# Scores and weighted sums of a cross attention in plain float32 on tiles of TensorE, in place of products of high and low parts

## The reference, cut to what matters

```
q = query @ Wq.T + bq;  k = ctx @ Wk.T + bk;  v = ctx @ Wv.T + bv      # 16 heads of 32
scores = einsum('bhqd,bhkd->bhqk', q, k) / sqrt(32)
s = where(scores >= 0, scores + 1, 1 / (1 - scores))                   # "stablemax"
attn = s / sum(s, axis=-1)
context = einsum('bhqk,bhkd->bhqd', attn, v)
out = context @ Wo.T + bo
```

## Time and profile before

| | |
|---|---|
| median of 3 runs | 1409.66 us (1409.51 to 1411.08) |
| the profiled execution's own time | 1411.17 us |
| its span, first to last instruction | 1409.4 us |
| PE busy | 1381.0 us, 98% |
| DVE busy | 902.0 us, 64% |
| ACT busy | 810.5 us, 58% |
| POOL busy | 417.1 us, 30% |
| mean granted TensorE clock | 0.993 |

### The profile page before, as it was taken

The page is one execution under the profiler, slowest core; times in us unless marked ns, Lnnn a source line. Parts: engine busy times, 40 slices in busy tenths (PEclk is TensorE's granted clock), DMA queues, the critical chain, the costliest instruction groups (busy, mean ns, idle before and its releaser), DMA issues.

```text
span 1409.4 us, 23502 instructions
## 1 busy us (share of the span) xinstructions
PE 1381.0 (98%) x9278; PEld 1243.1 (88%) x9278; DVE 902.0 (64%) x1491; ACT 810.5 (58%) x1453; POOL 417.1 (30%) x214
## 2 busy tenths in 40 slices
PE   8999999999999999999999999989999999999998
PEld 6999999989889989789998988879898999989997
DVE  5556766756766766766675676575676644645565
ACT  4666667657556755756765756564654435545443
POOL 2344444353344444434435333420003101001000
PEclk9999999999999999999999999999999999999999
DMA  6120111111121111011101111085454669999991
GB/s 221 63 71 27 35 34 31 31 65 46 31 72 31 31 64 60 16 61 42 31 31 64 46 31 65 31 330 184 152 189 149 212 216 348 339 366 338 352 392 51
DMA packets 34855, 174.41 MB, mean 124 GB/s; under 512 B 6155, under 2 KB 8363, under 8 KB 18485
## 3 DMA queue, kind: packets, MB, share of 16 engines
q1 hardware_dynamic: 32996, 168.10, 33.2%
q0 software_dynamic: 1744, 4.76, 1.1%
HBM read 166.78 MB, written 6.06 MB: 123 GB/s over the span
## 4 chain that ended last, share of the span: by engine, by line
PE 88%; DVE 6%; ACT 4%; issue 1%; DMA 1%; PEldq 0%; SPq 0%; DVEq 0%; PEld 0%; ACTq 0%
PE bank L700 18%; PE bank L688 17%; PE bank L1017 10%; PE bank L720 10%; PE bank L1034 8%; PE bank L874 6%; PE po L733 6%; PE po L891 6%; DVE tt L1297 1%; PE bank L791 1%; PE bank L755 1%; PE bank L836 1%; DVE sa L1305 1%; ACT tt L1178 1%; DVE sa L1310 1%
## 5 line engine op out<-in xcount | busy, mean ns | idle before, releaser
L554 POOL TENSOR_TENSOR xn<-xn,tt 128x1024 f32<-128x1024 f32 x96 | 237.5, 2474 | 461.1 <-DVE sa L1310 461.1
L1405 DVE TENSOR_TENSOR wsl<-ring,wsh 128x2048 fp32r<-128x2048 f32 x72 | 165.0, 2291 | 112.6 <-ACT wsh L1118 112.5
L1278 DVE SCALAR_TENSOR_TENSOR kl<-bank,bkt,kh 128x256 fp32r<-128x256 f32 (+1 forms) x190 | 93.6, 493 | 200.9 <-ACT kh L1069 200.7
L688 PE MATMUL bank<-cxh,wkh 128*128 128x256 f32 (+1 forms) x752 | 215.5, 287 | 3.2 <-DVE va L1285 3.2
L688 PE MATMUL bank<-cxl,wkh 128*128 128x256 f32 (+1 forms) x752 | 215.6, 287 | 0.0
L688 PE MATMUL bank<-cxh,wkl 128*128 128x256 f32 (+1 forms) x752 | 215.4, 286 | 0.0
L1173 ACT ACTIVATE tt<-bank 128x512 f32<-128x512 f32 (+1 forms) x208 | 124.3, 599 | 84.5 <-PE bank L720 78.7
L700 PE MATMUL bank<-wvh,cxh 128*128 128x512 f32 (+1 forms) x416 | 165.1, 397 | 1.3 <-DVE kl L1278 1.3
L1118 ACT CAST wsh<-ring 128x2048 fp32r<-128x2048 f32 x72 | 137.4, 1908 | 46.6 <-PE po L891 23.1
L700 PE MATMUL bank<-wvl,cxh 128*128 128x512 f32 (+1 forms) x416 | 163.7, 394 | 0.0
L700 PE MATMUL bank<-wvh,cxl 128*128 128x512 f32 (+1 forms) x416 | 163.3, 392 | 0.0
(11 more groups left out here) (252 smaller groups left out, 2938.7 us busy)
## 6 DMA issues: line engine op xcount, KB each, us to landing
ring<-in_w SPq DMA_DIRECT2D x112, 1024.0 KB, 6.8
ctxt<-in_ctx SPq DMA_DIRECT2D x40, 512.0 KB, 3.5
ctxt<-in_ctx SPq DMA_DIRECT2D x8, 642.0 KB, 4.0
wqt<-in_wo SPq DMA_DIRECT2D x4, 1024.0 KB, 5.7
wqt<-in_aq SPq DMA_DIRECT2D x4, 1024.0 KB, 6.5
wqt<-in_ap_ SPq DMA_DIRECT2D x4, 1024.0 KB, 6.5
yrows<-K SPq DMA_DIRECT2D x1, 2048.0 KB, 8.7
tt<-in_wk SPq DMA_DIRECT2D x2, 512.0 KB, 5.4
```

Source lines behind the costliest of these rows:

```text
L554: e.tensor_tensor(dacc[0:kn, y, :], dacc[0:kn, y, :], tt[0:kn, w, :], ALU.add).then_inc(s["da_pool"], 1)
L688: m = e.matmul(dst[:, 0:n], (wkh, wkl)[a][:, c, g * P:(g + 1) * P], (cxh, cxl)[b][:, u, c, 0:n], start=(c == 0 and x_ == 0), stop=(c == 3 ...
L1405: e.tensor_tensor(wsl[m % 3][:], ring[slot(unit_split(m))][:], wsh[m % 3][:].bitcast(F32), ALU.subtract).then_inc(s["wl_dve"], 1)
```

## The change

- Keys, values and queries are kept as plain float32 (`kk`, `va`, `qb`); their high and low parts and the instructions of ACT and DVE that made them go. DVE reads key and value banks in one instruction each (`keys`, `values`), ACT writes the queries.
- Scores: two products for each group, of 64 rows each (two heads, 128 columns), the one on rows 0 to 63 into bank `scb[n % 2][0]`, the other on rows 64 to 127 into `scb[n % 2][1]`. There are two pairs of score banks; a chunk waits for the reading of the chunk two before.
- Weighted sums: for each group four products of 32 weight columns (one head) with 64 columns, each into its own 32 rows of one bank, `pob[b % 2]`. They read `tt` itself, so `sa` and its splitting go. `batch_low` and `batch_out` go; `normalised` reads the bank.
- `tt` has three buffers. POOL's sum waits for `f_dve`.
- Order on PE: scores, `attended` (both batches in one slot), `shared_up`, weighted sums, denominators, all key groups, values. The last two chunks' values come one slot later than before. The 18 and 36 products on ones go.
- The first three expert loads are issued in slot 92 in place of behind the loop, the first two splits in slots 100 and 103. Buffers are laid out anew for this.

```diff
@@ scores (pe)
-                for hb in range(2):
-                    if n:
-                        e.wait_ge(s["f_dve"], 2 * (n - 1) + hb + 1)
...
-                    for g in (2 * hb, 2 * hb + 1):
-                        dst = scb[hb][0:kn, 256 * (g % 2):256 * (g % 2) + 256]
-                        for x_, (a, c) in enumerate(three):
-                            m = e.matmul(dst, (kh, kl)[a][:, u, g, k * P:k * P + kn], (qbh, qbl)[c][:, b % 2, g, :],
-                                         start=(x_ == 0), stop=(x_ == 2))
-                    m.then_inc(s["s_pe"], 1)
+                if n >= 2:
+                    e.wait_ge(s["f_dve"], 2 * (n - 2) + 2)
...
+                for g in range(4):
+                    if k == 0:
+                        e.wait_ge(s["proj_read"], use["k", i, g] + 1)
+                    for j in range(2):
+                        r = slice(64 * j, 64 * j + 64)
+                        m = e.matmul(scb[n % 2][j][0:kn, P * g:P * g + P], kk[r, u, g, k * P:k * P + kn],
+                                     qb[r, b % 2, g, :], start=True, stop=True)
+                        if g == 3:
+                            m.then_inc(s["s_pe"], 1)
@@ weighted (pe)
-                if head and b:
-                    e.wait_ge(s["out_dve"], 8 * b)
-                for hb in range(2):
-                    e.wait_ge(s["sl_dve"], 2 * n + hb + 1)
-                    for p_ in (2 * hb, 2 * hb + 1, 2 * hb + 4, 2 * hb + 5):
-                        m = e.matmul(po[:, 256 * p_:256 * p_ + 256], va[0:kn, n % VR, P * p_:P * p_ + P],
-                                     sa[0:kn, w, 256 * p_:256 * p_ + 256], start=(head and p_ % 2 == 0),
-                                     stop=(tail and p_ % 2 == 1), skip_group_check=True)
+                e.wait_ge(s["f_dve"], 2 * n + 2)
+                if head and b >= 2:
+                    e.wait_ge(s["cr_dve"], normalised_by(b - 2))
+                for g in range(4):
+                    for h in range(4):
+                        m = e.matmul(pob[b % 2][32 * h:32 * h + 32, 64 * g:64 * g + 64],
+                                     va[0:kn, n % VR, P * g + 32 * h:P * g + 32 * h + 32],
+                                     weights_of(tt[0:kn, n % TR, :], g, h), start=(head and g == 0),
+                                     stop=(tail and g == 3), skip_group_check=True)
@@ order of a slot (pe)
+                if tile(n, 9) is not None:
+                    for b in range(2):
+                        attended(tile(n, 9), b)
+                if NCH <= n < NCH + 2 * NSH:
+                    shared_up(n - NCH)
+                if 1 <= n < NCH + 1:
+                    weighted(n - 1)
+                for b in finished(n)[0]:
                     denominators(b)
-                if n == NCH:
-                    warm(36, pj[use["v", NCH - 1] % 2])
-                if 1 <= n < NCH + 1 and (n - 1) % PER:
-                    weighted(n - 1)
-                for i, g in late:
+                for i, g in early + late:
                     keys(i, g)
@@ act: before the three operations on tt
-                    if n >= 2:
-                        e.wait_ge(s["da_pool"], n - 1)
+                    if n >= TR:
+                        e.wait_ge(s["da_pool"], n - TR + 1)
+                        e.wait_ge(s["p_pe"], n - TR + 1)
@@ vector
+            def keys(i, g):
...
+                e.tensor_scalar(kk[:, u, g, 0:n], key_bank(i, g)[:, 0:n], bkt[:, g:g + 1], None,
+                                ALU.add).then_inc(s["proj_read"], 1)
...
-                    weights_hi(n, 0)
-                    weights_lo(n, 0)
@@ normalised (vector)
-                e.tensor_tensor(cU[:, y, gs, :], cU[:, y, gs, :], rd, ALU.mult).then_inc(s["cr_dve"], 1)
+                sums = pob[y][:, 0:256].rearrange("p (g q) -> p g q", g=4)
+                e.tensor_tensor(cU[:, y, gs, :], sums[:, gs, :], rd, ALU.mult).then_inc(s["cr_dve"], 1)
```

More of the change, by code:

```diff
@@ L138, in projections @@
             if tile(n, d) is not None:
[L139 to L142, removed]
+                uses.append((what, tile(n, d)))
+        if tile(n, 9) is not None:
+            uses += [("o", tile(n, 9), b) for b in range(2)]
+        uses += [("d", b) for b in finished(n)[0]]
+        uses += [("k", i, g) for i, g in early + late]
         if values_in(n) is not None:
@@ L413, in sync @@
                                 ).then_inc(s["yz_in"], 16)
+                if n == NCH - 12:
+                    for m in range(3):
+                        load_shared(m)
                 t = tile(n, 0)
@@ L946, in pe @@
                     turn_attention(tile(n, 8))
-                if tile(n, 9) is not None:
-                    attended(tile(n, 9), 0)
-                if tile(n, 10) is not None:
-                    attended(tile(n, 10), 1)
                 if tile(n, 11) is not None:
@@ L1144, in act @@
                 root(0, t)
-            for g in range(4):
-                keys_hi(0, g)
             turned(0, bank[2])
@@ L1185, in act @@
                         e.activation(tt[0:kn, w, r], tt[0:kn, w, r], ACT.Exp, scale=-1.0).then_inc(s["ex_act"], 1)
-                for i, g in late:
-                    keys_hi(i, g)
-                if ending(n, 1) is not None:
-                    batch_low(ending(n, 1))
                 for i in range(2, NPART):
@@ L1494, in vector @@
             e.tensor_copy(kio[:], iotai[:, P:P + 120].rearrange("p (k e) -> p k e", e=8)).then_inc(s["iota_dve"], 1)
-            for h in range(4):
-                queries_lo(0, h)
-            values_lo(0)
-            values_lo(1)
+            values(0)
+            values(1)
             count = [0]
@@ L1591, in vector @@
                 early, late = key_groups(n)
-                if 1 <= n < NCH - 1:
-                    values_lo(n + 1)
+                if n and values_in(n - 1) is not None:
+                    values(values_in(n - 1))
                 t = tile(n, 0)
@@ L1632, in vector @@
                         split_lo(t)
-                for b, part in finished(n)[0]:
-                    if part and b < NB - 1:
-                        batch_out(b, part)
+                if tile(n, 9) is not None:
+                    for b in range(2):
+                        attended(tile(n, 9), b)
+                for b in finished(n)[0]:
+                    denominators(b)
                 for i, g in early:
-                    keys_lo(i, g)
-                for b in finished(n)[1]:
-                    denominators(b)
+                    keys(i, g)
                 if n < NCH:
```

266 lines of the change are left out of this document (83 added, 183 removed).

## The result

The changed kernel takes 1334.62 us in the median (1333.59 to 1335.17, 4 runs) against 1410.37 us (4 runs) for the kernel before on the same chip: a ratio of 0.9461, 95% interval 0.9444 to 0.9477, 75.8 us less. The forecast was 1332 us. The profiled span is 1333.5 us against 1409.4.

A forecast was written before the change was run, and what follows sets the result against it. PE was taken as the bound, busy 98% of the span. Savings of 53 (slots) + 4 (a) + 10 (b) + 11 (c) = 78 us, and 1.5 from profiled run to median, took 1411.2 to 1332 us; 8-in-10 range 1306 to 1375.

The forecast's parts named there:

- The price of a slot: Chunk loop on PE: scores, weighted sums and form changes take 1.86 us instead of 2.37; 0.51 saved, 53 us over 104.
- rival 4: Form changes: row tiles change form without emptying and streaming alone counts; 0.25 us a slot, 26 us more gained, 1306; chance 0.06.
- rival 1: Scores: row tiles share the weight-load path, 16 loads in turn, 1.81 us a slot; 1427 us in all; chance 0.12.
- Rival 2: Weighted sums: small products paced by starts 0.025 us apart, 0.80 instead of 0.45 us a slot; 1368 us; chance 0.14.
- (a): Slots behind a finished batch: value products no longer wait for DVE's additions of sum parts; 0.6 us in 7 batches, 4 us.
- (b): Attended products of tiles 0 to 2, moved behind the scores: wait and half clock go, 3.4 us three times, 10 us.
- (c): Transition from chunk loop to experts: idle time, products on ones and half clock, 12.3 us, go; 11 us saved.
- rival 3: Chain through ACT and DVE ends last, 7.8 us instead of 4.5; sums wait 0.4 us a slot; 1372 us; chance 0.05.

The follow-up runs named there:

- attended_first: Against the kernel after, the two attended products of a tile (tiles 0 to 2) stand ahead of the chunk's scores again, both in one slot: 1335.88 us.
- third_early: Against the kernel after, tile 2's normalised rows are made in slot 95 and turned in slot 96, not slots 104 and 105: 1329.21 us.

## Why the prediction was right

**The price of a slot** was right in each part: rounds of 0.112 (0.113 said) and 0.056 us, changes of 0.20, 0.11 and 0.20 (the gaps above, and 21.4 us for 104 more of 0.20, which also refutes rival 4), 7.49 us a slot. The decisive choice, that row tiles overlap like the column tiles of L745, holds; rival 1 is refuted by the pairs, and by the 56 us that their separation costs. It was not the form alone that brought the gain but also the order of the loops: with the two loops of the sums exchanged, all of it but 2 or 3 us is gone. The prediction did not ask for the order; that the kernel had the good one is luck as far as the prediction goes. Rival 2's floor of 0.025 us between starts does not bind across tiles, which start 0.007 us apart. By the page "TensorE: Matmul & The Clock Gate" of the Trainium skill (Part 3, The mechanism) a load overlaps products only in other row groups: the trace after disagrees again, its rounds of 0.056 hold a load of a column tile and a product, both on all 128 rows.

**(a), the reading of `po`**: right. The slot behind a finished batch went from 8.58 to 7.49 us, 0.58 beyond the saving of each slot, 4 us in all.

**(b), attended products**: 10 us said, 14 measured. The wait and the half clock went as said, but for another reason than the place of the products, and the 1.72 us of streaming was priced too high. The two slots around them took 22.60 us (starts of scores at 356.89 and 379.49), now 16.27 (335.66 and 351.93); less 1.02 for the slots and 0.58 of (a) that is 4.7 us a tile. PE of after in order of time:

```profile
343.14 1.16 PE L692 MATMUL bank<-qb,kk 64*128 64x128 f32 x16
344.13 1.03 PE L804 MATMUL bank<-xaT,V 64*128 64x512 f32 x4
345.09 0.65 PE L706 MATMUL po<-tt,va 128*32 128x64 f32 x32
346.10 0.38 PE L662 MATMUL bank<-cxh,wkh 128*128 128x256 f32 x1 [0.36 <-DVE xa L1295]
```

All four records lie within 1.03 us where 1.72 of streaming had been counted: the two batches' products stand on rows 0-63 and 64-127 and write two banks, so they are a pair of row tiles themselves. In the kernel before they could not be one, as the second waited for its bank. The wait went because DVE now reads the value bank directly and not behind ACT's copy, in whatever place the products stand (`attended_first`); that they were moved is worth 0.4 us for each tile, about 1 in all. The half clock behind them (1.7 us each) is gone too, and no experiment here brought it back.

**(c), the transition**: 11 us said, 5 measured (7.0 less 2.0 that belong to its four slots). This is the step of the prediction that failed: I laid out the slots by the chain of scores, but left out the turning of tile 2's rows for the gates, which stands at the head of slot 105 on PE, ahead of the expert product. PE, POOL and DVE of after, each in order of time, and then the busy time of the stretch around the turning:

```profile
848.06 0.65 PE L706 MATMUL po<-tt,va 65*32 65x64 f32 x32 [0.62 <-DVE tt L1225]
854.83 1.09 PE L750 MATMUL bank<-ident,xa 128*128 128x128 f32 x4 [6.12 <-POOL xa L540]
...
850.33 4.36 POOL L540 TENSOR_SCALAR xa<-xres,mv,rstd 128x512 f32<-128x512 f32 x1
...
848.94 3.55 DVE L1320 TENSOR_TENSOR wsl<-ring,wsh 128x2048 fp32r<-128x2048 f32 x1 [1.03 <-ACT wsh L1068]
```

```profile
852.80:859.50 6.70, 4.67 (x22) 4.70 (x23) 3.89 (x4) 0.04 (x1) 1.89 (x1) 0.50 1.02 410
```

PE waits 6.12 us for rows that POOL makes in its own order behind its last sum. During this wait, at 852.8, the clock falls to half for 6.8 us; PE has work in the last 4.7 of them, so 2.4 us are lost, against 1.7 there before. Before, POOL made these rows at the same point and ended at 933.81, but PE itself came to the turning only at 934.04, with its idle time spread over earlier waits and the products on ones. The wait did not go; it moved to what came next in the queue. `third_early` shows that this was the missing part. Without the turning in its way the clock stayed at full, PE waited 0.6 and 1.4 us for DVE, and the transition took 25.9 us, 14.3 less than before. Less 2.0 for its slots and 0.4 that the turning costs in slot 95 (7.94 in place of 7.50) that is 11.9, where 11 had been said.

**Not said**: the denominators now follow the sums in the same form, so in their seven slots one change in and out is saved: 8.77 to 7.92, 0.34 beyond the slot's saving, 2.4 us. The start came 0.35 us earlier. The slots with wide key groups won 0.43 to 0.46 in place of 0.51, 1.1 us lost, and the experts took 1.2 us more.

The sum: 53.0 + 4.1 + 14.2 + 5.0 + 2.4 + 0.35 - 1.1 - 1.2 = 76.8, against 75.9 between the spans. Not told apart in it are slots with pieces of the self-attention, of which three (11.00 to 10.93 us) won only 0.07. The total was 2 to 3 us from the forecast with two errors of opposite sign, +4 in (b) and -6 in (c): the price of a slot was right by its reasons, and that the rest came out so near was luck.

The chain through ACT and DVE was no bound (rival 3): for before it was estimated at 4.5 us from the last scores to `f_dve`. In after DVE's second weight operation ends at 167.87 for scores that began at 162.63 and took 1.16, so 4.1 us, and PE needs it at 171.2.

## What to carry to other kernels

Price a matrix product on part of the array by rounds: in these runs products in different tiles of rows or columns counted once where neighbours in the program's order lay in different tiles, so make the tile the innermost loop. Add 0.1 to 0.2 us for each change between forms, and group work of one form (0.2 us here for sums set apart, 0.34 for denominators). When waits are taken out ahead of a handover, go down each engine's queue past the next few instructions, since the first one that hangs on an engine with its own order inherits the wait.

## What the runs showed of the hardware that was not expected

- A tile takes in three records ahead of the one that runs, and products go out in the program's order. With eight records of one tile ahead of the next tile's, the next tile's first record starts 5 to 7 ns behind the fifth, for two row tiles and for four column tiles alike; with blocks of four it starts 14 ns behind the first, and only the second block costs a round. So a bad order costs 56 us in place of 73 to 93, and 74 in place of 125 to 140. This is read from the single records of three orders; no run changed the number of records in another way.
- Two products of different lines of code, an attended one on rows 64-127 and scores on rows 0-63, overlapped as well.
- DVE and POOL held each other up where a DVE operation had both operands in SBUF. DVE's split (2048 elements) takes 2.28 us alone, and 3.86, 3.55 and 3.60 when it starts during POOL's sum; each time its end is the sum's end plus 2.28, within 0.15 us. A small DVE sum (L1353) starts beside a sum of POOL in all 14 of its places in after, takes 1.01 to 1.03 and ends 0.14 to 0.16 us behind POOL; in before the same operation (L1452) took 0.29. It goes the other way round as well: in before POOL's last sum starts 0.15 us behind a split and takes 4.36 in place of the 2.35 of after, and POOL's row operation takes 4.36 when it starts during a split and 2.12 in slot 95 of `third_early`. POOL, then DVE of after in order of time, and below DVE, then POOL of before:

```profile
160.46 2.39 POOL L528 TENSOR_TENSOR xn<-xn,tt 128x1024 f32<-128x1024 f32 x1 [3.04 <-DVE tt L1225]
162.00 1.01 DVE L1353 TENSOR_TENSOR xT<-xT,bvt 128x128 f32<-128x128 f32 x1
...
927.23 2.28 DVE L1405 TENSOR_TENSOR wsl<-ring,wsh 128x2048 fp32r<-128x2048 f32 x1
...
927.38 4.36 POOL L554 TENSOR_TENSOR xn<-xn,tt 65x1024 f32<-65x1024 f32 x1 [2.19 <-DVE sa L1310]
```

  DVE operations with one operand in PSUM were not held up: the low part of the values in before (L1285) took 0.69 us in the 94 places beside a sum of POOL and in the 10 without. No run took POOL's sum away, so this is read from traces and not shown by an edit. The page "SBUF — State Buffer" of the Trainium skill (SBUF: two separate sides) states it as a lock on a pair of ports that VectorE with two SBUF inputs and a GpSimd operation that reads SBUF take in turn, each for the whole instruction. These numbers agree but for one: POOL's row operation ends at 854.69 by its record, and DVE's next split started at 853.85 and took 2.28 us all the same.
- A 1.04 us gap between half-array products did not lower the clock; 6.1 us without any product did: the clock fell about 4 us after the last product had ended, for 6.8 us.
